# One GroupNorm evaluation per half-unit for both convolution stages of a ViT tokenizer on Trainium2

## The chip, the cores and the metric

The kernel runs on one core of one Trainium2 chip (trn2). The metric is the device time of one execution in microseconds (us); lower is better. The names of the engines in the rows are PE (TensorE matrix products), PEld (its weight loads), DVE (VectorE), ACT (ScalarE), POOL (GpSimd) and SP (the queue that issues DMAs).

## What is computed

A tokenizer over 784 patches (16 images, 7 x 7 patches of 3 x 16 x 16 pixels) feeds a small transformer. Only the tokenizer is touched here:

```python
x = _conv2d(x, conv1_w, conv1_b)              # 3 -> 64 channels, 3x3
residual = x
x = _group_norm(x, gn1_g, gn1_b)              # 32 groups of 2 channels, per patch
x = jax.nn.gelu(x, approximate=False)
x = _conv2d(x, rconv1_w, rconv1_b)            # 64 -> 64 channels, 3x3: the big one
x = _group_norm(x, gn2_g, gn2_b)
x = jax.nn.gelu(x, approximate=False)
x = _conv2d(x, rconv2_w, rconv2_b)
x = residual + x
x = _conv2d(x, proj_w, proj_b, stride=P, pad=0)   # 16x16 patch -> 192 numbers
```

The second residual convolution and the projection are folded into one weight (stage "fold"), so that what stands in the loop is: conv1, group norm 1, GELU 1, big convolution (`rconv1`), group norm 2, GELU 2, projection. The residual path is handled by another small product in the second half of the program.

## The kernel before, in words

**Tiling.** A unit is `U = 8` patches, a half is `Q = 4` patches; there are `UNITS = 98` units, so 196 halves, k = 2u + q with q = 0 or 1. Channels lie twice on the 128 partitions (odd and even rows of a patch), so a half of one stage is a PSUM bank of 128 x 512 numbers: `c1[q]` for conv1, `rc[p][q]` for the big convolution (p is the parity of the unit). Fourteen units make a group (`GU`), and there are seven groups. While group g runs through the convolutions, TensorE also projects group g-1: from the fifth half of a group on, every half carries 10 or 12 products of the projection (`project`), cut into 12 chunks of weights of which six units' worth are loaded again by DMA in every group. Group 0 has no projection beside it; the projection of group 6 stands alone after the loop. After it comes the second part of the program (`build_tail`), which the change leaves alone.

**What each engine does for a half k** (its emission or slot k); all five streams are written out by hand and only semaphores tie them together:

- TensorE, `emit`: 15 pairs of 64-column products of the big convolution of half k (lines 506 and 507; the two of a pair run side by side), with the projection's products (562, 566) strewn between them by `woven`. After pair 6 it waits for the copies of half k (`s_dup`), after pair 7 comes `means` of stage 1 for half k+3 (line 550, four small products that average the statistics of two channels), after pair 10 `conv1` of half k+4 into `c1[q]` (540, 541), which waits until GELU 1 of half k+2 has read that bank (`s_g1`), and after pair 13 of an even half `means` of stage 2 for the unit before. An emission starts only when `s_sp1` (split of half k done) and `s_g2` (GELU 2 of half k-4 done, the bank `rc` free) allow it.
- VectorE, `slot`: `channel_stats` of conv1 of half k+3 (four `bn_stats`, 777), `moments` of it (784 to 789), `channel_stats` of the big convolution of half k-1, `read_means` (793), `split1` of half k+2 (804 casts GELU 1 to the high 16 bits, 806 subtracts to get the low ones), in even halves `moments` of stage 2 over a whole unit, `split2` (813), in even halves `read_means` of stage 2.
- GpSimd, `norm(stage, ...)`: six or seven tiny operations in a chain (362, 363, 365, the power -0.5 in 367, 369, 371, 373) that turn averages into a scale `gsc` and a shift `gsh`. Per unit: stage 1 of four columns, stage 2 of eight columns, stage 1 of four columns.
- ScalarE: `gelu1` of half k+2 (420), then `gelu2_at` of half k-3 (429) and `hi2` (437, the high 16 bits of GELU 2).
- SP: per unit two loads of the im2col rows (254), per half four copies of `hst` into `acts` (274), and in groups 1 to 6 one chunk of the projection's weights (283).

All the statistics, averages, scales and shifts of stage 1 lie in buffers 0 and 1 (of four columns, in turn by half), those of stage 2 in buffers 2 and 3 (of eight columns, in turn by unit):

```python
N1, N2 = (0, 1), (2, 3)
wide = (Q, Q, U, U)
```

Of the kernel before, what the change touches and what calls it, by code (L numbers as in the profile page):

```python
# [28 lines left out]
HALF = 8 * P  # L29
# [22 lines left out]
MID = 48  # L52

# [15 lines left out]
def build_front(nc, a, emb, xs, ts, wrd):  # L69
# [9 lines left out]
    with ExitStack() as ctx:  # L79
# [25 lines left out]
        N1, N2 = (0, 1), (2, 3)  # L105
        wide = (Q, Q, U, U)
        bn6 = [sb(f"bn6_{s}", [128, w, 6]) for s, w in enumerate(wide)]
        ms = [sb(f"ms_{s}", [128, 2, w, 2]) for s, w in enumerate(wide)]
        msq = [sb(f"msq_{s}", [128, w, 2]) for s, w in enumerate(wide)]
        mst = [sb(f"mst_{s}", [128, 2, w]) for s, w in enumerate(wide)]  # L110
        tmp = [sb(f"tmp_{s}", [128, 5, w]) for s, w in enumerate(wide)]
        gsc = [sb(f"gsc_{s}", [128, w]) for s, w in enumerate(wide)]
        gsh = [sb(f"gsh_{s}", [128, w]) for s, w in enumerate(wide)]
        wid = sb("wid", [128, 2, 3, U])
# [57 lines left out]
        s_ms, s_st, s_rd = ([sem(f"{n}{s}") for s in (1, 2)] for n in ("moments", "group_means", "means_read"))  # L172
        s_dch, s_pch, s_sh = ([sem(f"{n}{s}") for s in (1, 2)] for n in ("dve_chain", "pool_chain", "affine"))
# [170 lines left out]
        def _(pool):  # L344
# [39 lines left out]
            norm(0, 0, 0)  # L384
            norm(0, 1, 1)
            norm(0, 0, 2)
            over_groups(pool, lambda g, b, first: over_units(pool, g, pair, first))
            norm(1, N2[1], UNITS - 1)

        @block.scalar  # L390
        def _(act):
# [48 lines left out]
            def group(g, b, first):  # L440
                def pair(u0, j, first, head):
                    for p in range(2):
                        u = u0 + p
                        for q in range(2):

                            gelu1(2 * u + 2 + q, q)
                            if first and 2 * p + q < 3:
                                continue
                            if head and 2 * p + q == 3:
                                act.wait_ge(s_pj, 1 if first else g)  # L450
                            uu, qq, pp = (u - 2, 1, p) if q == 0 else (u - 1, 0, 1 - p)
                            gelu2_at(uu, qq, pp)
                            old = head and 2 * p + q < 3
                            hi2(uu, qq, 1 - b if old else b, slot2(j, p, q, old))
# [1157 lines left out]
```

## Time and profile before

| | |
|---|---|
| median of three runs | 1846.43 us (1845.34 to 1847.88) |
| profiled execution, its own time | 1844.27 us |
| its span, first to last instruction | 1842.5 us |
| TensorE busy | 1513.2 us, 82% |
| VectorE busy | 1124.3 us, 61% |
| ScalarE busy | 850.0 us, 46% |
| GpSimd busy | 884.6 us, 48% |
| first conv1 of the loop to the last one (196 halves) | 269.4 to 1491.2 us |

The span is what the trace covers, the profiled execution's own time lies 1.8 us above it, and the median of the runs 2.2 us above that. Some 1222 us of it are the loop over the halves. An engine that is busy for 82% of the span is not thereby the bound: one has to see what the idle time of each engine in the loop waits for. Times of rows are in us from the start of the span, and one matrix product's own time (0.38 us) includes its way through the array, so the rate is read from start to start.

### The profile page before, as it was taken

What the parts mean: (1) busy time and instruction counts of PE and PEld (TensorE: products, weight loads), DVE (VectorE), ACT (ScalarE), POOL (GpSimd) and SP (SyncE); (2) the same over time, 40 slices, a digit from 0 to 9 for tenths busy, and PEclk for the clock granted to TensorE, in tenths of its full rate; (3) what the DMA queues carried; (4) which work ended last, traced back from release to release, by engine and by line L of the source; (5) the groups of instructions that cost most, each with busy time, mean ns of one, the idle gap of its engine ahead of it and who ended that gap; (6) DMA issues with size and microseconds to landing.
All of it is one profiled execution on the core that took longest, in us unless ns stands there. A gap on an engine that the chain in (4) does not pass through costs nothing. (4 is left out here: it accounts for less than half of the span.)

```text
span 1842.5 us, 45180 instructions
## 1 busy us (share of the span) xinstructions
PE 1513.2 (82%) x13782; PEld 1018.5 (55%) x13782; DVE 1124.3 (61%) x4307; ACT 850.0 (46%) x2118; POOL 884.6 (48%) x2190
## 2 busy tenths in 40 slices
PE   6879967666888788878888887888788857788999
PEld 3434423333666466646665665566566647656657
DVE  8533437767766766767767766667667653347330
ACT  1212225665555555555555555555555530243441
POOL 2000026666666666656666666666666640123410
PEclk9989979999999999989999999999999988786999
DMA  5643353323444344334434443444344465700000
GB/s 163 197 115 92 94 198 82 79 72 98 113 122 108 99 126 117 98 106 112 122 92 116 124 114 84 122 113 120 94 116 122 115 165 158 159 1 1 1 1 14
DMA packets 117232, 190.78 MB, mean 104 GB/s; under 512 B 18251, under 2 KB 86282, under 8 KB 116940
## 3 DMA queue, kind: packets, MB, share of 16 engines
q1 hardware_dynamic: 117068, 188.60, 37.5%
q8 instruction: 102, 1.67, 0.3%
q14 instruction: 62, 0.51, 0.1%
HBM read 103.34 MB, written 21.30 MB: 68 GB/s over the span
## 5 line engine op out<-in xcount | busy, mean ns | idle before, releaser
L506 PE MATMUL rc<-sb_acts,sb_rwd 128*64 128x512 f16 x1764 | 565.8, 393 | 4.7 <-DMA sb_acts<-sb_hst 4.7
L507 PE MATMUL rc<-sb_acts,sb_rwd 128*64 128x512 f16 x1764 | 566.9, 394 | 0.0
L506 PE MATMUL rc<-sb_acts,sb_rwl 128*64 128x512 f16 x1176 | 368.3, 395 | 111.9 <-ACT sb_g2f L429 78.8
L420 ACT ACTIVATE sb_f32q<-c,sb_gsh,sb_gsc 128x128 f32<-128x128 f32 x792 | 298.6, 458 | 308.8 <-POOL sb_gsh L373 308.8
L429 ACT ACTIVATE sb_g2f<-rc,sb_gsh,sb_gsc 128x128 f32<-128x128 f32 x784 | 296.5, 469 | 216.7 <-POOL sb_gsh L373 202.3
L367 POOL TENSOR_TENSOR sb_tmp<-sb_tmp,sb_half_neg 128x4 f32<-128x4 f32 (+1 forms) x297 | 371.0, 1249 | 23.5 <-POOL sb_tmp L365 0.5
L507 PE MATMUL rc<-sb_acts,sb_rwl 128*64 128x512 f16 x1176 | 369.7, 396 | 0.0
L813 DVE TENSOR_TENSOR sb_arena<-sb_g2f,sb_arena 128x512 f32 (+1 forms) x196 | 135.8, 693 | 326.6 <-ACT sb_arena L437 313.1
L362 POOL TENSOR_TENSOR sb_tmp<-sb_mst 128x4 f32<-128x4 f32 (+1 forms) x297 | 71.6, 241 | 545.3 <-DVE sb_mst L793 545.2
L562 PE MATMUL pj<-sb_wall,sb_arena 128*64 128x384 f16 x1792 | 306.0, 339 | 20.4 <-DMA sb_wall<-w_lo 11.3
L566 PEld LDWEIGHTS pj<-sb_wall,sb_arena 128*64 128x64 f16 x1792 | 213.3, 225 | 72.3 <-issue 2.4
L566 PE MATMUL pj<-sb_wall,sb_arena 128*64 128x192 f16 x1792 | 234.6, 248 | 0.0
L562 PEld LDWEIGHTS pj<-sb_wall,sb_arena 128*64 128x64 f16 x1792 | 210.1, 221 | 44.1 <-DMA sb_wall<-w_lo 12.8
L506 PEld LDWEIGHTS rc<-sb_acts,sb_rwl 128*64 128x64 f16 x1176 | 126.2, 110 | 177.5 <-issue 144.8
L481 PE MATMUL rc<-sb_acts,sb_arena 128*128 128x512 f16 x864 | 196.5, 385 | 29.3 <-DVE sb_acts L694 29.3
L506 PEld LDWEIGHTS rc<-sb_acts,sb_rwd 128*64 128x64 f16 x1764 | 170.8, 111 | 57.7 <-DMA sb_acts<-sb_hst 5.6
L550 PE MATMUL st<-sb_ms,sb_grp 128*64 128x16 f32 (+1 forms) x1188 | 86.0, 218 | 121.3 <-DVE sb_ms L789 120.4
L777 DVE BATCH_NORM_STATS2 sb_bn<-c 128x6 f32<-128x128 f32 x796 | 175.6, 283 | 7.2 <-issue 5.5
L550 PEld LDWEIGHTS st<-sb_ms,sb_grp 128*64 128x64 f32 x1188 | 66.0, 138 | 201.1 <-DVE sb_ms L789 125.0
L777 DVE BATCH_NORM_STATS2 sb_bn<-rc 128x6 f32<-128x128 f32 x784 | 173.8, 284 | 0.6 <-PE rc L507 0.6
L507 PEld LDWEIGHTS rc<-sb_acts,sb_rwd 128*64 128x64 f16 x1764 | 170.4, 111 | 0.5
L481 PEld LDWEIGHTS rc<-sb_acts,sb_arena 128*128 128x128 f16 x864 | 81.9, 97 | 135.5 <-issue 34.6
(161 smaller groups left out, 2310.2 us busy)
## 6 DMA issues: line engine op xcount, KB each, us to landing
sb_acts<-sb_hst SPq DMA_DIRECT2D x792, 78.8 KB, 2.1
sb_wall<-w_lo SPq DMA_DIRECT2D x56, 528.0 KB, 3.9
sb_im<-x_planes SPq DMA_DIRECT2D x202, 136.5 KB
sb_wall<-w_lo SPq DMA_DIRECT2D x28, 480.0 KB, 3.7
sb_f32q<-in_proj SPq DMA_DIRECT2D x12, 576.0 KB, 4.1
sb_arena<-in_proj SPq DMA_DIRECT2D x12, 576.0 KB, 4.4
w_lo<-sb_arena SPq DMA_DIRECT2D x1, 6144.0 KB, 17.3
scratch_fold<-sb_wall SPq DMA_DIRECT2D x48, 123.8 KB
```

The costliest lines, as they stand in the source:

```text
L362: ch.did(gp.tensor_tensor(t1, mean, mean, ALU.mult))
L367: ch.did(gp.tensor_tensor(t5, t3, half_neg[:, 0:w], ALU.pow))
L420: ins = nc.scalar.activation(g1f[:, q * Q + m, :], c1[q][:, m * HALF:(m + 1) * HALF], ACT.Gelu, bias=gsh[q][:, m:m + 1], scale=gsc[q][:, m ...
L429: ins = nc.scalar.activation(g2f[:, q * Q + m, :], rc[p][q][:, m * HALF:(m + 1) * HALF], ACT.Gelu, bias=gsh[s][:, q * Q + m:q * Q + m + 1] ...
L481: last = nc.tensor.matmul(out, w[:, wp, 3 * t + m, :], v[:, xp, t:t + 8, m * Q:(m + P) * Q], start=(n == 0), stop=(n == 17))
L506: nc.tensor.matmul(out[0:CH, :], w_odd, x_odd, start=(n == 0), stop=(n == 14))
L507: yield nc.tensor.matmul(out[CH:128, :], w_even, x_even, start=(n == 0), stop=(n == 14))
L550: last = nc.tensor.matmul(st[64 * h:64 * h + 64, 0:4 * wide[s]], grp[:, 64 * h:64 * h + 64], ms[s][:, :, :, :].rearrange("p a b k -> p (a ...
L562: last = nc.tensor.matmul(pj[at:at + 64, 0:2 * E], g2[:, b, 0, k:k + 64, n], both, start=(n == 0), stop=False)
L566: last = nc.tensor.matmul(pj[at:at + 64, 0:E], g2[:, b, 1, k:k + 64, n], whi[:, n, :], start=False, stop=(n == HALF - 1))
L777: v.bn_stats(bn6[s][:, at + m, :], src[:, m * HALF:(m + 1) * HALF]).then_inc(s_dch[stage_], 1)
L813: v.tensor_tensor(lo, src, hi, ALU.subtract).then_inc(s_sp2, 1)
```

## The change

One set of two buffers, each eight columns wide, takes the place of the four. Buffer s holds in columns 0 to 3 the statistics of conv1 of half n = k+3 and in columns 4 to 7 those of the big convolution of half n-4 = k-1. `moments`, `means`, `read_means` and `norm` run once a half over the eight columns; `wid` and `wid2` hold the parameters of stage 1 in the first four columns and of stage 2 in the last four.

- VectorE's slot becomes: statistics of the big convolution of half k-1, statistics of conv1 of half k+3, `moments`, `split2` of half k-3, `read_means`, `split1` of half k+2.
- TensorE's emission has one `means`, after pair 10 (`MEANS_AT`), and `conv1` after pair 13 (`CONV1_AT`).
- GpSimd has one eight-wide `norm` a half, with two more waits ahead of the write to `gsc` (until the GELUs that read that buffer's old values are done).
- ScalarE does `gelu2_at` and `hi2` of half k-3 ahead of `gelu1` of half k+2; GELU 2 of a half reads columns 4 to 7 of buffer q and waits for norm 2u+q+5.
- At the start the parameters are spread with a few more small VectorE operations, and the first three norms are eight wide.

```diff
+MEANS_AT, CONV1_AT = 10, 13
...
-            def norm(stage_, s, n):
+            def norm(n, s, guard=True):
...
-                pool.wait_ge(s_rd[stage_], n + 2)
+                pool.wait_ge(s_rd, n + 2)
...
+                if guard:
+                    pool.wait_ge(s_g1, n - 1)
+                    pool.wait_ge(s_g2, n - 1)
                 ch.did(gp.tensor_tensor(gsc[s][:, :], t5, gam, ALU.mult))
...
-                    norm(0, 1, 2 * u + 3)
-                    if not (first and p == 0):
-                        norm(1, N2[1 - p], u - 1)
-                    norm(0, 0, 2 * u + 4)
+                    for q in range(2):
+                        norm(2 * (u0 + p) + q + 3, 1 - q)
...
             def gelu2_at(u, q, p):
-                s = N2[p]
-                act.wait_ge(s_sh[1], u + 1)
+                act.wait_ge(s_sh, 2 * u + q + 5)
...
+                                gelu2_at(uu, qq, pp)
+                                old = head and 2 * p + q < 3
+                                hi2(uu, qq, 1 - b if old else b, slot2(j, p, q, old))
                             gelu1(2 * u + 2 + q, q)
...
-            def means(stage_, s, n, other):
-
-                pe.wait_ge(s_ms[stage_], n + 1)
-                pe.wait_ge(s_rd[stage_], n + 1)
-                pe.wait_ge(s_rd[1 - stage_], other + 1)
+            def means(n, s):
+
+                pe.wait_ge(s_ms, n + 1)
+                pe.wait_ge(s_rd, n + 1)
...
                 pe.wait_ge(s_dup[p][q], 64 * (pairs_done + 1))
-                woven(1)
-                means(0, N1[1 - q], 2 * u + q + 3, u - (q == 0) if k2 else 0)
-                woven(3)
+                woven(MEANS_AT - 6)
+                means(2 * u + q + 3, 1 - q)
+                woven(CONV1_AT - MEANS_AT)
                 if q == 0:
                     pe.wait_ge(s_im[p], 32 * (pairs_done + 2))
                 pe.wait_ge(s_g1, 2 * u + q + 3)
                 conv1(q, p)
-                woven(3)
-                if q == 0 and k2:
-                    means(1, N2[1 - p], u - 1, 2 * u + q + 4)
-                woven(2).then_inc(s_rc, 1)
+                woven(15 - CONV1_AT).then_inc(s_rc, 1)
...
+                    if seen:
+                        dve.wait_ge(s_rc, k)
+                        channel_stats(1 - q, rc[p][0] if q == 1 else rc[1 - p][1], Q)
                     dve.wait_ge(s_c1, k + 5)
-                    channel_stats(0, N1[1 - q], c1[1 - q], 0)
-                    moments(0, N1[1 - q], 7 * (k + 3) + 4)
...
-                    read_means(0, N1[1 - q], k + 3)
-                    split1(k + 2, q, 1 - p, pair_at + 1)
-                    if q == 0 and n2:
-                        moments(1, N2[1 - p], 11 * (u - 1) + 8)
-
+                    channel_stats(1 - q, c1[1 - q], 0)
+                    moments(k + 3, 1 - q, 11 * k + 25 if seen else 25)
                     if not (first and p == 0) and not (first and p == 1 and q == 0):
                         old = head and 2 * p + q < 3
                         split2(k - 3, 1 - q, 1 - b if old else b, slot2(j, p, q, old))
-                    if q == 0 and n2:
-                        read_means(1, N2[1 - p], u - 1)
+                    read_means(k + 3, 1 - q)
+                    split1(k + 2, q, 1 - p, pair_at + 1)
```

How the rows stand on the engines that the prediction speaks of. First VectorE, in the last loop over units, an even half before (777 is `bn_stats`, 784 to 789 `moments`, 793 `read_means`, 804 and 806 `split1`, 813 `split2`):

```order
L777 BN_STATS sb_bn_1<-c_1 128x6 x4
...
L784 TENSOR_SCALAR sb_ms<-sb_bn_1,sb_par 128x8
...
L777 BN_STATS sb_bn_2<-rc 128x6 x4
...
L793 TENSOR_REDUCE sb_mst<-st 128x8
L804 CAST sb_hst<-sb_f32q 128x4x8x16
L806 TENSOR_TENSOR sb_acts<-sb_f32q,sb_hst 128x4x8x16
...
L784 TENSOR_SCALAR sb_ms<-sb_bn_2,sb_par 128x16
...
L813 TENSOR_TENSOR sb_arena<-sb_g2f,sb_arena 128x512
L793 TENSOR_REDUCE sb_mst<-st 128x16
```

And the same place now (770 is `bn_stats`, 777 to 782 `moments`, 786 `read_means`, 797 and 799 `split1`, 806 `split2`):

```order
L770 BN_STATS sb_bn_1<-rc 128x6 x4
...
L770 BN_STATS sb_bn_1<-c_1 128x6 x4
...
L777 TENSOR_TENSOR sb_ms<-sb_bn_1,sb_wid 128x16
...
L806 TENSOR_TENSOR sb_arena<-sb_g2f,sb_arena 128x512
...
L786 TENSOR_REDUCE sb_mst<-st 128x16
...
L797 CAST sb_hst<-sb_f32q 128x4x8x16
L799 TENSOR_TENSOR sb_acts<-sb_f32q,sb_hst 128x4x8x16
```

The second `moments` and the second `read_means` are gone, the statistics of the big convolution stand first, and `split2` moved ahead of `read_means`, `split1` to the end.

TensorE in an even half with projection, before, around the two products of `means` and `conv1` (550 is `means`, 540 `conv1`, 506 and 507 a pair, 562 and 566 the projection):

```order
L550 MATMUL st<-sb_ms,sb_grp 64x16 x2
L506 MATMUL rc<-sb_acts,sb_rwd 64x512
L507 MATMUL rc<-sb_acts,sb_rwd 64x512
...
L540 MATMUL c_0<-sb_im,sb_w1s 64x512
L541 MATMUL c_0<-sb_im,sb_w1s 64x512
...
L550 MATMUL st<-sb_ms,sb_grp 64x32 x2
```

And now (546 is `means`, 537 `conv1`, 503 and 504 a pair, 558 and 562 the projection):

```order
L546 MATMUL st<-sb_ms,sb_grp 64x32 x2
L503 MATMUL rc<-sb_acts,sb_rwd 64x512
L504 MATMUL rc<-sb_acts,sb_rwd 64x512
...
L558 MATMUL pj<-sb_wall,sb_arena 64x384 x2
...
L537 MATMUL c_0<-sb_im,sb_w1s 64x512
L538 MATMUL c_0<-sb_im,sb_w1s 64x512
```

One `means` stands where two stood, three pairs later than the first of them, and `conv1` three pairs later too.

## Rows read from the trace of the kernel before

**Rows 1.** TensorE's line 541 by window: busy us (x halves), granted clock, DMA:
```profile
269.30:438.00 168.70, 10.97 (x28) 3.15 (x29) 0.99 0.30 78
269.30:1491.30 1222.00, 75.12 (x196) 21.23 (x196) 0.99 0.40 107
```
**Rows 2.** Waits of TensorE in the loop: total us, times, longest:
```profile
PE st L550 <- DVE sb_ms L789: 111.2, 181, 4.1
PE rc L506 <- ACT sb_g2f L429: 78.8, 59, 2.2
```
**Rows 3.** Timeline, TensorE, one unit: start, length, instruction [idle before <-releaser]:
```profile
1001.56 0.38 PE L506 MATMUL rc<-sb_acts,sb_rwl 128*64 128x512 f16 x1 [0.55 <-issue]
...
1008.00 0.38 PE L506 MATMUL rc<-sb_acts,sb_rwl 128*64 128x512 f16 x1
...
1010.31 0.25 PE L550 MATMUL st<-sb_ms,sb_grp 128*64 128x16 f32 x4
...
1011.32 0.38 PE L540 MATMUL c<-sb_im,sb_w1s 108*64 108x512 f16 x1
...
1012.47 0.41 PE L506 MATMUL rc<-sb_acts,sb_rwd 128*64 128x512 f16 x1
...
1013.10 0.26 PE L566 MATMUL pj<-sb_wall,sb_arena 128*64 128x192 f16 x2
1014.24 0.40 PE L506 MATMUL rc<-sb_acts,sb_rwl 128*64 128x512 f16 x1 [0.88 <-ACT sb_g2f L429]
```
**Rows 4.** The same unit on VectorE:
```profile
1002.49 0.70 DVE L813 TENSOR_TENSOR sb_arena<-sb_g2f,sb_arena 128x512 f32 x1 [3.00 <-ACT sb_arena L437]
...
1004.02 0.23 DVE L784 TENSOR_SCALAR sb_ms<-sb_bn,sb_par 128x8 f32<-128x8 f32 x1
...
1004.58 0.88 DVE L777 BATCH_NORM_STATS2 sb_bn<-rc 128x6 f32<-128x128 f32 x4
...
1005.45 0.42 DVE L804 CAST sb_hst<-sb_f32q 128x512 f16<-128x512 f32 x1
1005.91 0.71 DVE L806 TENSOR_TENSOR sb_acts<-sb_f32q,sb_hst 128x512 f16<-128x512 f32 x1
...
1007.95 0.18 DVE L793 TENSOR_REDUCE sb_mst<-st 128x16 f32<-128x32 f32 x1
```
**Rows 5.** The same unit on ScalarE:
```profile
1001.60 0.63 ACT L437 ACTIVATE sb_arena<-sb_g2f 128x512 f32 x1
...
1012.50 1.51 ACT L429 ACTIVATE sb_g2f<-rc,sb_gsh,sb_gsc 128x128 f32<-128x128 f32 x4 [2.23 <-POOL sb_gsh L373]
```
**Rows 6.** The same unit on GpSimd:
```profile
1006.16 0.52 POOL L365 TENSOR_TENSOR sb_tmp<-sb_mst,sb_tmp 128x4 f32<-128x4 f32 x1
...
1008.60 0.20 POOL L362 TENSOR_TENSOR sb_tmp<-sb_mst 128x8 f32<-128x8 f32 x1
1008.76 0.20 POOL L363 TENSOR_TENSOR sb_tmp<-sb_mst,sb_wid 128x8 f32<-128x8 f32 x1
...
1012.26 0.20 POOL L373 TENSOR_TENSOR sb_gsh<-sb_wid,sb_tmp 128x8 f32<-128x8 f32 x1
```
**Rows 7.** GpSimd, the last norm of the loop, VectorE idle beside it:
```profile
1499.00 0.20 POOL L363 TENSOR_TENSOR sb_tmp<-sb_mst,sb_wid 128x8 f32<-128x8 f32 x1
...
1501.84 0.20 POOL L373 TENSOR_TENSOR sb_gsh<-sb_wid,sb_tmp 128x8 f32<-128x8 f32 x1
```
**Rows 8.** Timeline, SP's queue, four copies of one half and the copy kind's landing:
```profile
1023.61 2.38 SPq L274 DMA_DIRECT2D sb_acts<-sb_hst  x4
```
**Rows 9.** The page, DMA issues: count, KB each, median us from issue to landing:
```profile
sb_acts<-sb_hst SPq DMA_DIRECT2D x792, 78.8 KB, 2.1
```
**Rows 10.** Timeline, VectorE: first operation of group 5, behind its loop's branch:
```profile
1144.15 0.89 DVE L777 BATCH_NORM_STATS2 sb_bn<-c 128x6 f32<-128x128 f32 x4 [2.70 <-issue]
```
**Rows 11.** Timeline, TensorE, from the loop's last emission to the last projection:
```profile
1497.72 0.43 PE L550 MATMUL st<-sb_ms,sb_grp 128*64 128x32 f32 x4 [4.66 <-DVE sb_ms L789]
1507.08 0.62 PE L562 MATMUL pj<-sb_wall,sb_arena 128*64 128x384 f16 x2 [8.94 <-DVE sb_arena L813]
```

More of the change, by code:

```diff
@@ L103, in build_front @@
         par = sb("par", [128, 7])
[L105 to L114, printed above, removed]
+        bn6 = [sb(f"bn6_{s}", [128, U, 6]) for s in range(2)]
+        ms = [sb(f"ms_{s}", [128, 2, U, 2]) for s in range(2)]
+        msq = [sb(f"msq_{s}", [128, U, 2]) for s in range(2)]
+        mst = [sb(f"mst_{s}", [128, 2, U]) for s in range(2)]
+        tmp = [sb(f"tmp_{s}", [128, 5, U]) for s in range(2)]
+        gsc = [sb(f"gsc_{s}", [128, U]) for s in range(2)]
+        gsh = [sb(f"gsh_{s}", [128, U]) for s in range(2)]
+        wid = sb("wid", [128, 3, U])
+        wid2 = sb("wid2", [128, U, 2])
         zeros = sb("zeros", [128, U])
@@ L444, in pair @@
                         for q in range(2):
-                            gelu1(2 * u + 2 + q, q)
[L447 to L454, printed above, removed]
+                            if not (first and 2 * p + q < 3):
+                                if head and 2 * p + q == 3:
+                                    act.wait_ge(s_pj, 1 if first else g)
+                                uu, qq, pp = (u - 2, 1, p) if q == 0 else (u - 1, 0, 1 - p)
+                                gelu2_at(uu, qq, pp)
+                                old = head and 2 * p + q < 3
+                                hi2(uu, qq, 1 - b if old else b, slot2(j, p, q, old))
+                            gelu1(2 * u + 2 + q, q)
                 pair(g * GU, 0, first, True)
@@ L576, in emit @@
             def emit(u, q, p, g, b, first, pairs_done, s_idx=None):
-                k2 = not (first and p == 0)
                 pe.wait_ge(s_sp1, 2 * u + q + 1)
@@ L645, in _ @@
             conv1(1, 0)
-            means(0, 0, 0, 0)
-            means(0, 1, 1, 0)
+            means(0, 0)
+            means(1, 1)
             pe.wait_ge(s_im[1], 32)
@@ L650, in _ @@
             conv1(0, 1)
-            means(0, 0, 2, 0)
+            means(2, 0)
             pe.wait_ge(s_g1, 2)
@@ L654, in _ @@
             over_groups(pe, group)
-            means(1, N2[1], UNITS - 1, 2 * UNITS + 3)
+            means(2 * UNITS + 3, 1)
             for c in range(NCH):
@@ L862, in _ @@
             dve.wait_ge(s_c1, 2)
[L863 removed]
+            channel_stats(0, c1[0], 0)
             moments(0, 0, 4)
             dve.wait_ge(s_c1, 3)
[L866 to L869 removed]
+            channel_stats(1, c1[1], 0)
+            moments(1, 1, 11)
+            read_means(0, 0)
+            read_means(1, 1)
             split1(0, 0, 0, None)
             dve.wait_ge(s_c1, 4)
[L872 to L874 removed]
+            channel_stats(0, c1[0], 0)
+            moments(2, 0, 18)
+            read_means(2, 0)
             split1(1, 1, 0, None)
@@ L885, in _ @@
             dve.wait_ge(s_rc, K)
-            channel_stats(1, N2[1], rc[1][1], Q)
-            moments(1, N2[1], 11 * (UNITS - 1) + 8)
-            read_means(1, N2[1], UNITS - 1)
+            channel_stats(1, rc[1][1], Q)
+            dve.wait_ge(s_c1, K + 5)
+            channel_stats(1, c1[1], 0)
+            moments(K + 3, 1, 11 * K + 25)
+            read_means(K + 3, 1)
             for k in (K - 3, K - 2, K - 1):
```

85 lines of the change are left out of this document (35 added, 50 removed).

## The prediction

> **What bounds the kernel now.** I read the windows by line first: 28 conv1 of group 0 lie 168.7 us apart in all, 196 of the whole loop 1222 us [rows 1], so a half costs 6.0 us without a projection beside it and 6.2 over all. Adding the projection's products costs almost nothing, so TensorE's work is not the bound. The list of waits says who is: 111 us for the moments of VectorE and 79 us for GELU 2, in the loop alone [rows 2]. The timeline of one unit gives TensorE's own pace. An odd half runs without a wait from 1008.00 to the last product at 1013.10 and 0.09 beyond, 5.19 us, and the whole unit takes 1001.56 to 1014.24 = 12.68 [rows 3]. The even half has two projection products less (384 and 192 columns, 0.16 and 0.08 us at the granted 2.4 GHz, share 0.99 [rows 1]), hence 4.95. The four chunks of ten in twelve take another 0.24 a unit off: on average 10.06 a unit, **5.03 a half**, against some 6.3 spent.
>
> What closes the loop is one ring a unit, and it is seen by following who ends each wait: `hi2` at 1001.60 [rows 5]; `split2` at 1002.49, which VectorE stood 3.00 us for; statistics, moments, split and at last the stage 2 `read_means` at 1007.95 [rows 4]; the eight-wide norm 1008.60 to 1012.46 [rows 6]; GELU 2 at 1012.50 to 1014.01 [rows 5]; TensorE's next even half at 1014.24, 0.88 idle for just that [rows 3]. From 1001.60 to the next `hi2`, 0.12 behind 1014.01, is 12.5 us: the period. It passes VectorE, GpSimd and ScalarE one after the other, so each is idle half the time and yet together they set the pace.
>
> **What is removed and added.** Per unit one `moments`, one `means` and one `read_means` of three go, and two norms of four columns and one of eight become two of eight. What counts is not their busy time but where the ring now closes. I set out one half, t = 0 at the start of emission k, P the period.
>
> 1. The big convolution of half k-1 is done near t = 0.1. Statistics of it and of conv1, 0.88 each, with hand-overs 1.8; moments 0.56 (1004.02 to 1004.58) [rows 4]. The averages can start at 2.5. TensorE gets there after ten pairs: `conv1` stood behind ten pairs at 1011.32, 3.32 from 1008.00, and 0.08 of that is the old `means` (1010.31, four products, next start 0.08 on) [rows 3]: 3.24. The wait for moments goes, with 0.7 to spare.
> 2. `means` 0.25 and 0.04, `read_means` 0.18 [rows 3, 4]: read at 3.71. `split2` (0.70) lies ahead of it, from 2.4 to 3.1, free: its input was ready long before, see 4.
> 3. The norm, N. Bare it takes 1499.00 to 1502.04 and 0.16 for its first step, **3.20** [rows 6, 7]. In the ring it took 1008.60 to 1012.46, **3.86** [rows 6], because VectorE's `split1` ran into it: line 365 takes 0.52 instead of 0.20 when it meets line 806 (1005.91 to 1006.62) and ends 0.06 behind it [rows 4, 6]. Now `split1` starts together with the norm or up to 0.4 us behind, so something of this stays; the power, which is more than half of N, outlasts it. I take N = 3.4, ends 3.2 and 3.9.
> 4. GELU 1 starts 0.04 behind the norm and takes 1.51, GELU 2 of half k-4 another 1.5, `hi2` 0.63 [rows 5]. ScalarE has 3.9 us of work a half, below P. GELU 1 of half k+2 is done at 3.76 + N + 1.55 - P = 8.7 - P, so at 3.6 for P = 5.07. GELU 2 is done 1.5 later, in emission k, and TensorE wants it at emission k+2: the 79 us go.
> 5. `conv1` comes behind pair 13: the row at 1012.47, less the old `conv1` (0.23), 4.24 [rows 3]. Needed: GELU 1 by then. From `means` to the next half's `conv1` there are P + 1.00; the chain takes 0.29 + 0.18 + 0.05 + N + 0.04 + 1.51 + 0.05 = N + 2.12. So **P >= N + 1.12**: 4.52 at N = 3.4, 4.98 at 3.86. Below 5.03, but closely.
> 6. VectorE's own ring: `read_means` of half n, norm, GELU 1, `split1` (1.17 with its cast at 1005.45 to 1006.62), then statistics 1.8, moments 0.56, `split2` 0.61, the next but one `read_means`: 0.18 + 0.05 + N + 0.04 + 1.51 + 0.05 + 1.17 + 1.8 + 0.56 + 0.61, that is 5.97 + N for two halves [rows 4 to 7]. **P >= 4.7** at N = 3.4; 4.6 to 4.9 for its ends.
> 7. The copies of a half: the cast ends near 4.6 in slot k-2, four issues take 2.38, the last lands 2.1 after its issue [rows 8, 9], so at 9.1; emission k wants them behind pair 6, near 2P + 1.9 = 12. 2.9 us to spare. The im2col loads and chunks share the queue, and a unit still has 10 us.
>
> So with the projection beside it a half becomes TensorE's: 5.03, and I take **5.07** since single halves may meet point 5. Without it (28 halves of group 0, four at the head of each later group, 52 in all) TensorE would need less than 4 us, and point 6 gives **4.7**.
>
> **The sum.** 143 x 5.07 = 725; 52 x 4.7 = 244; two passes over the outer loop's branch, where VectorE stood 2.70 us [rows 10] and nothing covers it: 5.4; for the token outputs at six group ends and some microseconds at 1.2 GHz behind them I allow 9. In all 984, against 1222 [rows 1]: 238 less. Outside the loop: from the end of the last emission (1497.72 - 4.66 = 1493.06) to the first product of the last projection (1507.08) are 14.0 us [rows 11]; the new order has one GELU 2 left there instead of two: 1.8 + 0.56 + 0.5 + N (bare) 3.2 + 1.51 + 0.8 + 0.8 = 9.2, 4.8 less. At the start three norms grow from four columns to eight; the two that stand in line cost some 2 us. 1844.3 - 238 - 4.8 + 2 = 1603.5, and the median of the runs lay 2.2 above the profiled execution: **1606**. With N = 3.2 and 5.03 a half it is 1595; with N = 3.9 (4.94 and 5.1) it is 1623.
>
> **A row that speaks against it.** Point 3 rests on one reading: a GpSimd operation that meets line 806 only ends late, it does not lose the whole overlap. No row shows the power beginning under `split1`. Were it held for the full cast and subtraction, 0.42 + 0.71 [rows 4], then N = 4.33. The Trainium skill, GPSIMD Engine Reference, section "Key points", says that GpSimd shares its SBUF interfaces with VectorE and contends with instructions of a 2-port mode or with two SBUF inputs, which both parts of `split1` may be. The 0.52 agrees that there is contention; how much of a long operation it costs no row here shows. By the page, with the whole overlap lost, the sum would be that of the first rival below.
>
> **The rivals.**
> - *The norm is held for all of `split1`.* N = 4.33, so P = 5.45 with the projection and (5.97 + 4.33) / 2 = 5.15 without: 779 + 268 + 14 = 1061, 161 less. **1683.** For it: the collision is now in every half. Against it: a held operation ends 0.06 behind VectorE's, so its reading and its work were done under the hold.
> - *Another wait takes the place.* The queue of SP is the candidate: a copy has 2.9 us to spare, and all 16 DMA engines will be busier (0.40 of the span now [rows 1]) in less time. If the copies came late by so much that P stayed at 5.75, the loop would give back 0.68 x 143 = 97 us; at 6.2, and 5.2 without the projection, 162 + 26 = 188: **1703 to 1794**. Against it: the margin of point 7.
> - *Slower: the merged norm stands on the path of both stages.* GELU 1 now waits for statistics of the big convolution that it never needed. If not only `split1` but all of VectorE's work held GpSimd (0.42 + 0.71 + 0.70 + 1.76 + 0.56 = 4.15), N would be 7.35, P = 8.5 and 6.7: 1215 + 348 + 14, **about 2195**. It is slower than before from N = 5.3 on. Against it: line 362 took 0.20 at 1008.60 [rows 6], where VectorE, done with `read_means` at 1008.13 [rows 4], was at the next half's `bn_stats`, so these don't hold it.
> - *No change.* A ring that I don't see closes at 6.2. The order of rows shows that the old one is cut, so this is a residue.
>
> **How the numbers follow.** The forecast (1583 to 1630) 0.67; norm held (1630 to 1695) 0.16; another wait (1695 to 1840) 0.09; no change 0.02; slower 0.06. The likeliest is 1606. The range takes the first two cases, 1583 to 1695. Faster by over 0.2% (about what a measurement of this kernel can tell from none): 0.92; within it 0.02; slower 0.06.
>
> **What the changed kernel's profile would show.** Conv1 to conv1 5.0 to 5.2 us with the projection, even and odd halves nearly alike, and 4.6 to 4.9 in group 0; TensorE waits for neither moments nor GELU 2; GpSimd starts its norm each half near 3.8 us behind TensorE's start and takes 3.2 to 3.9; ScalarE has about 1.2 us idle a half. I am wrong at point 3 if the power row takes over 1.9 us; at point 5 if line 537 waits for GELU 1; at point 7 if the first pair behind pair 6 waits for a DMA; at point 1 if `means` still waits for moments.

## The result and the profile after

| | before | changed |
|---|---|---|
| median of four runs | 1847.16 us (1845.34 to 1849.16) | **1636.3 us** (1624.12 to 1637.54) |
| profiled execution, its own time / span | 1844.27 / 1842.5 us | 1635.12 / 1633.3 us |
| ratio to before, 95% interval | | 0.8843 (0.88 to 0.8887) |
| first conv1 of the loop to the last | 1222 us | 1012 us (271.5 to 1283.5) |

In a later session the same kernel took 1628.62 us, ratio 0.8853 (0.8824 to 0.8882). The time is inside the range, 30 us above the forecast of 1606. It lies in the band (1630 to 1695) that the prediction had set apart for its first rival with a chance of 0.16, 6 us above the forecast's own band, and not because that rival's mechanism came true; the later session's 1628.62 lies in the forecast's band.

The page of the changed kernel, busy time by engine and the landing of the copies (median in the last column, against 2.1 in [rows 9]):

```profile
PE 1467.2 (90%) x13394; PEld 1002.0 (61%) x13394; DVE 1086.1 (66%) x3830; ACT 837.3 (51%) x2118; POOL 713.5 (44%) x1511
...
sb_acts<-sb_hst SPq DMA_DIRECT2D x792, 78.8 KB, 2.6
```

Line 538 (conv1's second product) by window, the answer to [rows 1]: group 0, the whole loop, and a stretch with the projection. 28 halves now lie 141.7 us apart in all instead of 168.7, all 196 take 1012 instead of 1222:

```profile
271.40:413.10 141.70, 11.25 (x29) 3.03 (x29) 1.00 0.36 92
271.40:1283.40 1012.00, 76.96 (x195) 20.93 (x195) 0.99 0.48 129
900.00:990.00 90.00, 6.68 (x17) 1.82 (x17) 1.00 0.52 139
```

Waits of TensorE in the loop, the answer to [rows 2] (total us, times, longest). The 111 us for moments are 12.3, the 79 us for GELU 2 are gone; what is left is 37.7 us for GELU 1 at conv1, in 26 places, nearly all in group 0 and the group heads (the first four halves of a group, which have no projection yet). The list has only waits in which TensorE stood idle:

```profile
PE c L537 <- ACT sb_f32q L419: 37.7, 26, 1.6
PE st L546 <- DVE sb_ms L782: 12.3, 33, 1.3
PE rc L503 <- issue: 6.9, 2, 3.7
PE rc L503 <- DMA sb_acts<-sb_hst: 4.3, 12, 0.8
```

**With the projection** a half is nearly TensorE's own. From 900 to 960 us it was busy all of the 60.00 us at a granted clock of 1.00, and conv1 follows conv1 by 5.09 and 5.13 in turn. Even so, every second conv1 there was released by GELU 1:

```profile
908.73 0.41 PE L537 MATMUL c<-sb_im,sb_w1s 108*64 108x512 f16 x1
```
```profile
907.18 1.50 ACT L419 ACTIVATE sb_f32q<-c,sb_gsh,sb_gsc 128x128 f32<-128x128 f32 x4 [2.14 <-POOL sb_gsh L375]
```

GELU 1 ended at 908.68 and conv1 began 0.05 behind it, 1.08 behind `means` (907.65). All 66 such halves that I counted have this 0.05, and conv1 comes 1.11 behind `means` in them (median), 1.02 in the others, where GELU 1 ends 0.77 before it. The product ahead was still running, so this wait of 0.1 is in no list of idle time. GpSimd and VectorE there; start, length, instruction. The power (line 366) begins under the cast of `split1`, runs on under its subtraction and takes 1.70, against 1.64 where no 128x512 instruction of VectorE overlaps it:

```profile
908.94 1.70 POOL L366 TENSOR_TENSOR sb_tmp<-sb_tmp,sb_half_neg 128x8 f32<-128x8 f32 x1
...
908.71 0.43 DVE L797 CAST sb_hst<-sb_f32q 128x512 f16<-128x512 f32 x1 [0.57 <-ACT sb_f32q L419]
909.18 0.70 DVE L799 TENSOR_TENSOR sb_acts<-sb_f32q,sb_hst 128x512 f16<-128x512 f32 x1
```

The norm took 3.24 there (908.23 to 911.47) and 3.92 in the next half (913.42 to 917.34).

**In group 0** the steady halves take 4.2 or 4.3 and 5.9 us in turn, because only every second norm stands in the ring. GpSimd's norm of one half, and the next one's first step:

```profile
366.39 0.31 POOL L361 TENSOR_TENSOR sb_tmp<-sb_mst 128x8 f32<-128x8 f32 x1 [2.51 <-DVE sb_mst L786]
366.67 0.19 POOL L362 TENSOR_TENSOR sb_tmp<-sb_mst,sb_wid 128x8 f32<-128x8 f32 x1
366.94 0.53 POOL L364 TENSOR_TENSOR sb_tmp<-sb_mst,sb_tmp 128x8 f32<-128x8 f32 x1
367.55 1.64 POOL L366 TENSOR_TENSOR sb_tmp<-sb_tmp,sb_half_neg 128x8 f32<-128x8 f32 x1
...
369.84 0.71 POOL L375 TENSOR_TENSOR sb_gsh<-sb_wid,sb_tmp 128x8 f32<-128x8 f32 x1
370.67 0.20 POOL L361 TENSOR_TENSOR sb_tmp<-sb_mst 128x8 f32<-128x8 f32 x1
```

And VectorE over the same two halves, `read_means` to the next but one `read_means` (line 786):

```profile
366.13 0.18 DVE L786 TENSOR_REDUCE sb_mst<-st 128x16 f32<-128x32 f32 x1
366.23 0.42 DVE L797 CAST sb_hst<-sb_f32q 128x512 f16<-128x512 f32 x1
366.68 0.73 DVE L799 TENSOR_TENSOR sb_acts<-sb_f32q,sb_hst 128x512 f16<-128x512 f32 x1
...
369.80 0.69 DVE L806 TENSOR_TENSOR sb_arena<-sb_g2f,sb_arena 128x512 f32 x1 [0.17 <-issue]
...
372.30 0.43 DVE L797 CAST sb_hst<-sb_f32q 128x512 f16<-128x512 f32 x1 [1.71 <-ACT sb_f32q L419]
...
373.38 0.88 DVE L770 BATCH_NORM_STATS2 sb_bn<-rc 128x6 f32<-128x128 f32 x4
...
375.83 0.69 DVE L806 TENSOR_TENSOR sb_arena<-sb_g2f,sb_arena 128x512 f32 x1 [0.15 <-issue]
376.44 0.18 DVE L786 TENSOR_REDUCE sb_mst<-st 128x16 f32<-128x32 f32 x1
```

The ring of point 6 is there: 366.13 to 376.44 = 10.31 for two halves. Its parts are 0.26 to the norm, 4.16 norm, 1.75 to `split1`, 1.08, statistics 1.70, moments with the gap behind them 0.75, `split2` 0.61. Forecast were 0.23, 3.4, 1.60, 1.17, 1.80, 0.56, 0.61 = 9.37. The norm alone is 0.76 over, and its rows say why: three of its small steps, 0.20 each by themselves, took 0.31, 0.53 and 0.71, and each ends 0.05 or 0.06 behind a VectorE instruction of 128x512: the cast, the subtraction of `split1`, and `split2`. So `split1` took 0.44 from this norm, where 0.2 was forecast, and `split2` 0.51, where nothing was. The next norm (370.67 to 374.08) took 3.41, and TensorE did not wait for it.

**The end of the loop**, the answer to [rows 11]:

```profile
1287.64 0.31 PE L546 MATMUL st<-sb_ms,sb_grp 128*64 128x32 f32 x4 [3.16 <-DVE sb_ms L782]
1295.26 0.62 PE L558 MATMUL pj<-sb_wall,sb_arena 128*64 128x384 f16 x2 [7.32 <-DVE sb_arena L806]
```

From the last emission's end (1287.64 - 3.16) to the first product are 10.8 us instead of 14.0.

### The profile page after: what moved, and what is told of

It reads as the page before. It is cut to its first block and busy times, and to the rows that moved or that the text cites. A ratio compares the mean times of both kernels' runs of the same rounds, so it can differ in the third digit from the quotient of the medians.

```text
span 1633.3 us, 42631 instructions
## 1 busy us (share of the span) xinstructions
PE 1467.2 (90%) x13394; PEld 1002.0 (61%) x13394; DVE 1086.1 (66%) x3830; ACT 837.3 (51%) x2118; POOL 713.5 (44%) x1511
## 5 line engine op out<-in xcount | busy, mean ns | idle before, releaser
L366 POOL TENSOR_TENSOR sb_tmp<-sb_tmp,sb_half_neg 128x8 f32<-128x8 f32 x200 | 335.3, 1677 | 15.7
L558 PE MATMUL pj<-sb_wall,sb_arena 128*64 128x384 f16 x1792 | 300.8, 339 | 20.7 <-DMA sb_wall<-w_lo 13.4
L361 POOL TENSOR_TENSOR sb_tmp<-sb_mst 128x8 f32<-128x8 f32 x200 | 58.4, 292 | 530.5 <-DVE sb_mst L786 528.8
L562 PEld LDWEIGHTS pj<-sb_wall,sb_arena 128*64 128x64 f16 x1792 | 210.8, 226 | 75.6 <-issue 0.5
L558 PEld LDWEIGHTS pj<-sb_wall,sb_arena 128*64 128x64 f16 x1792 | 208.1, 223 | 41.2 <-DMA sb_wall<-w_lo 14.6
L562 PE MATMUL pj<-sb_wall,sb_arena 128*64 128x192 f16 x1792 | 230.9, 248 | 0.0
L503 PEld LDWEIGHTS rc<-sb_acts,sb_rwd 128*64 128x64 f16 x1764 | 180.4, 110 | 69.1 <-DMA sb_acts<-sb_hst 13.0
L504 PEld LDWEIGHTS rc<-sb_acts,sb_rwd 128*64 128x64 f16 x1764 | 180.3, 110 | 4.0
L806 DVE TENSOR_TENSOR sb_arena<-sb_g2f,sb_arena 128x512 f32 (+1 forms) x196 | 135.8, 693 | 28.8 <-issue 12.8
L797 DVE CAST sb_hst<-sb_f32q 128x512 f16<-128x512 f32 x198 | 85.3, 431 | 93.2 <-ACT sb_f32q L419 92.2
L799 DVE TENSOR_TENSOR sb_acts<-sb_f32q,sb_hst 128x512 f16<-128x512 f32 x198 | 141.1, 713 | 6.8
## 6 DMA issues: line engine op xcount, KB each, us to landing
w_lo<-sb_arena SPq DMA_DIRECT2D x1, 6144.0 KB, 17.3
```

What stands on the lines that cost most here:

```text
L366: ch.did(gp.tensor_tensor(t5, t3, half_neg[:, :], ALU.pow))
L503: nc.tensor.matmul(out[0:CH, :], w_odd, x_odd, start=(n == 0), stop=(n == 14))
L504: yield nc.tensor.matmul(out[CH:128, :], w_even, x_even, start=(n == 0), stop=(n == 14))
L558: last = nc.tensor.matmul(pj[at:at + 64, 0:2 * E], g2[:, b, 0, k:k + 64, n], both, start=(n == 0), stop=False)
L562: last = nc.tensor.matmul(pj[at:at + 64, 0:E], g2[:, b, 1, k:k + 64, n], whi[:, n, :], start=False, stop=(n == HALF - 1))
L797: v.tensor_copy(hi, src).then_inc(s_sp1h, 1)
```

## The experiments

Two theories came out of this. *Bounds*: with the projection a half takes the larger of TensorE's pace and N + 1.12 (point 5); without it, half of 5.97 + N (point 6). *Hold*: N is 3.2 plus what VectorE's 128x512 instructions take from it, and `split2` in its new place is one of them. The rivals were that something else (the copies, the clock, the places of `means` and `conv1`) sets those halves. The table has, worked out from the starts of conv1, the steady time of **two** halves in group 0 and with the projection. Each ratio is to the kernel before, timed again in the same session.

| kernel | group 0 | with projection | median us | ratio to before (95%) |
|---|---|---|---|---|
| before | 12.3 | 12.6 | 1847 | 1 |
| changed | 4.2 + 5.9 | 5.09 + 5.13 | 1636.3 | 0.8843 (0.88 to 0.8887) |
| e1, `split2` behind `read_means` | 10.05 | 5.13 + 5.58 | 1667.0 | 0.9044 (0.9003 to 0.9085) |
| e2, norm longer | 11.2 | 5.05 + 6.3 | 1735.8 | 0.9426 (0.9379 to 0.9473) |
| e3, before, stage 2 norm longer | 12.8 | 12.85 | 1880.86 | 1.0212 (1.0151 to 1.0273) |
| e4, earlier places | 10.4 | 5.44 + 5.44 | 1675.02 | 0.9103 (0.9058 to 0.9149) |
| e5, GELU 1 first | 17.3 | 8.6 + 8.7 | 2291.96 | 1.2437 (1.2372 to 1.2501) |
| e6, stage 1's columns first | 9.4 | 5.02 + 5.11 | **1602.33** | 0.871 (0.8675 to 0.8744) |
| e7, `split2` between statistics | 10.75 | 5.1 + 5.7 | 1675.43 | 0.9091 (0.9058 to 0.9123) |
| e8, e6 and e7 together | 10.25 | 5.0 + 5.25 | 1632.59 | 0.8852 (0.8818 to 0.8887) |
| e9, as e6, all on GpSimd | 9.85 | 5.0 + 5.1 | 1611.8 | 0.875 (0.8715 to 0.8786) |
| e10, e1 with conv1 at 14 | 10.0 | 5.0 + 5.3 | 1643.14 | 0.8902 (0.8863 to 0.8941) |

The changed kernel itself took 1636.3 us in one session and 1628.62 in another at nearly the same ratio (0.8843 and 0.8853), so a difference between medians of two sessions can be off by some 8 us.

### e1: split2 behind read_means

```diff
                     moments(k + 3, 1 - q, 11 * k + 25 if seen else 25)
+                    read_means(k + 3, 1 - q)
                     if not (first and p == 0) and not (first and p == 1 and q == 0):
                         old = head and 2 * p + q < 3
                         split2(k - 3, 1 - q, 1 - b if old else b, slot2(j, p, q, old))
-                    read_means(k + 3, 1 - q)
                     split1(k + 2, q, 1 - p, pair_at + 1)
```

> The changed kernel with one edit: VectorE's split2 stands behind read_means and ahead of split1, instead of ahead of read_means. Theory (split2 holds the norm of the half before and lies on VectorE's ring in the 52 halves without a full projection beside them): a half without projection falls from 5.06 to about 4.5 to 4.7 us, the norm there from 4.16 to about 3.7, halves with the projection stay at 5.1 since TensorE is their bound; in all about 20 us less than the changed kernel, 1610 to 1620. Rival (these halves are held by something else, the clock or the copies): no change, 1630 to 1640. Second rival (split2 now meets the start of every norm and only moves the hold, while split1 waits 0.6 longer): slower, 1640 to 1660.

Measured: 1667.0. The direction is that of the second rival, the size is past it. Group 0 gained some 0.15 in two halves; every second half with the projection went from 5.1 to 5.58, which the first theory had left out. GpSimd and VectorE there:

```profile
926.21 0.20 POOL L361 TENSOR_TENSOR sb_tmp<-sb_mst 128x8 f32<-128x8 f32 x1 [1.90 <-DVE sb_mst L786]
926.37 0.68 POOL L362 TENSOR_TENSOR sb_tmp<-sb_mst,sb_wid 128x8 f32<-128x8 f32 x1
...
927.46 2.10 POOL L366 TENSOR_TENSOR sb_tmp<-sb_tmp,sb_half_neg 128x8 f32<-128x8 f32 x1
...
926.29 0.69 DVE L806 TENSOR_TENSOR sb_arena<-sb_g2f,sb_arena 128x512 f32 x1 [0.16 <-issue]
...
927.37 0.70 DVE L799 TENSOR_TENSOR sb_acts<-sb_f32q,sb_hst 128x512 f16<-128x512 f32 x1
```

`split2` now meets the norm's start instead of its end (0.68 instead of 0.20), and `split1`, pushed back by it, meets the start of the power: 2.10 instead of 1.64. The norm took 926.21 to 930.59 = 4.38, and N + 1.12 = 5.50 against 5.58 measured. The hold was moved, not removed. TensorE waited for GELU 1 in 101 places instead of 26. So point 5's bound is real, and the changed kernel stood on it in every second half with the projection: 3.92 + 1.12 = 5.04 against 5.11.

### e2 and e3: a longer norm

e2 does one small step of the norm four times instead of once, 0.84 us more with the same result; e3 does so in the kernel before, in the stage 2 norm alone.

```diff
-                ch.did(gp.tensor_tensor(t3, sq, t1, ALU.subtract))
-                ch.wait()
+                for _ in range(4):
+                    ch.did(gp.tensor_tensor(t3, sq, t1, ALU.subtract))
+                    ch.wait()
```

> The changed kernel with the third step of GpSimd's norm (t3 = sq - t1, 8 columns, same result) done four times instead of once: each norm longer by three such steps, about 0.84 us from the distance of two steps in the trace (0.28). Theory (a half with the projection needs P = N + 1.12, a half without (5.97 + N) / 2 plus the hold): with N about 4.1 to 4.7, halves with projection go from 5.12 to 5.4 to 5.6, those without by 0.42, so 143 x 0.4 + 52 x 0.42, some 60 to 80 us more: 1695 to 1715. Rival (TensorE alone bounds the halves with projection and there is 0.8 to spare): only the 52 halves pay, 22 us: about 1658.

Measured: 1735.8, 99 us more, where the theory had 60 to 80. GpSimd's norm in one of the longer halves, and TensorE's wait behind it:

```profile
950.55 0.44 POOL L361 TENSOR_TENSOR sb_tmp<-sb_mst 128x8 f32<-128x8 f32 x1 [2.33 <-DVE sb_mst L787]
...
954.52 0.58 POOL L372 TENSOR_TENSOR sb_gsc<-sb_tmp,sb_wid 128x8 f32<-128x8 f32 x1 [0.22 <-POOL sb_tmp L367]
...
957.34 0.41 PE L538 MATMUL c<-sb_im,sb_w1s 108*64 108x512 f16 x1 [1.16 <-ACT sb_f32q L420]
```

This norm took 5.12 (to 955.67), since its later steps now meet `split2` (0.58): 5.12 + 1.12 = 6.24, measured 6.3. The next, 955.63 to 959.66, took 4.03, which asks for 5.15, and TensorE's own 5.05 to 5.1 was kept. Group 0 grew by 13.4 us over 28 halves, 0.48 each, where point 6 asks for half of 0.84, 0.42. The rival, slack of over 0.84 with the projection, is out.

> The kernel before with the same three extra steps (0.84 us) in the stage 2 norm alone, the eight-wide one of each unit; the result is the same. Theory (one ring a unit passes through that norm once and sets 12.5 us a unit): 98 units x 0.84 = 82 us more, about 1929. Rival (the ring is not what bounds the unit, the norm has slack): under 20 us more, 1847 to 1867.

Measured: 1880.86, 40 us more, between both; from two runs, 1.5% to 2.7% slower. The loop (1232 to 1261 us, from one conv1 ahead) took 29 of the 39 us between the two traces, 0.25 to 0.5 a unit. Some 2 lie before it, and most of the rest lies near the end, in `build_tail`, which this edit leaves alone: the granted clock was 0.82 and 0.84 in two stretches there (1759 to 1796 and 1796 to 1829 us), where the kernel before had 1.00 and 0.89 (1728 to 1758 and 1758 to 1790). So that part is no price of the norm. The ring of [rows 3 to 6] does pass through this norm, but the added 0.84 came through as 0.28 in it, because the power and the step behind it no longer meet `split1`, and the unit grew by about as much. Before (first row) one took 0.67, with the longer norm (second) 0.20:

```profile
936.04 0.67 POOL L369 TENSOR_TENSOR sb_gsc<-sb_tmp,sb_wid 128x8 f32<-128x8 f32 x1
```
```profile
968.65 0.20 POOL L370 TENSOR_TENSOR sb_gsc<-sb_tmp,sb_wid 128x8 f32<-128x8 f32 x1
```

The norm took 3.78 before (933.49 to 937.27) and 4.06 here (965.35 to 969.41), the unit 12.6 and 12.85.

### e4: earlier places

```diff
-MEANS_AT, CONV1_AT = 10, 13
+MEANS_AT, CONV1_AT = 7, 10
```

> The changed kernel with means behind pair 7 instead of 10 and conv1 behind pair 10 instead of 13 (MEANS_AT, CONV1_AT = 7, 10); the distance between them is the same. Theory (only the wait for moments, ready some 2.5 us into a half, is late against the earlier place at 2.3, and the chain from means to conv1 one half on is as long as before): 0 to 15 us more, 1636 to 1651. Rival (the places are essential: moments are later than 2.5, and each half then waits for them in the open): over 30 us more, above 1666.

Measured: 1675.02, 39 us more, the rival. A half with the projection takes some 5.4; the waits for moments in the loop rose from 12.3 to 45.9 us:

```profile
PE st L546 <- DVE sb_ms L782: 45.9, 57, 2.0
```

The expectation contradicted the prediction's own number. Point 1 gave moments 0.7 us to spare, and the changed kernel's trace has that (moments done at 912.13, `means` at 912.84: 0.71). Three pairs with their products are 0.96, so each half had to pay some 0.3, and it did.

### e5: ScalarE's old order

```diff
+                            gelu1(2 * u + 2 + q, q)
                             if not (first and 2 * p + q < 3):
...
                                 hi2(uu, qq, 1 - b if old else b, slot2(j, p, q, old))
-                            gelu1(2 * u + 2 + q, q)
```

> The changed kernel with ScalarE's old order in a half: GELU 1 first, then GELU 2 of half k-3 and its rounded copy (hi2). Theory (split2 stands ahead of read_means, so GELU 2 behind GELU 1 closes a ring of one half: read_means 0.2, norm 3.3, GELU 1 1.5, GELU 2 1.4, hi2 0.8, split2 0.6 and hand-overs): a half takes 7.9 us, the kernel 2100 to 2200, slower than before. Rival (point 4 of the prediction: GELU 2 has emissions to spare, so its place on ScalarE does not matter): within 0.5% of the changed kernel, 1628 to 1645.

Measured: 2291.96, the theory, past its 2100 to 2200: a half takes 8.6 instead of 7.9. The order of the two GELUs is worth some 655 us. VectorE, then ScalarE:

```profile
906.00 0.69 DVE L806 TENSOR_TENSOR sb_arena<-sb_g2f,sb_arena 128x512 f32 x1 [4.49 <-ACT sb_arena L435]
906.61 0.18 DVE L786 TENSOR_REDUCE sb_mst<-st 128x16 f32<-128x32 f32 x1
```
```profile
902.15 1.51 ACT L419 ACTIVATE sb_f32q<-c,sb_gsh,sb_gsc 128x128 f32<-128x128 f32 x4 [5.03 <-POOL sb_gsh L375]
903.54 1.52 ACT L427 ACTIVATE sb_g2f<-rc,sb_gsh,sb_gsc 128x128 f32<-128x128 f32 x4
905.18 0.64 ACT L435 ACTIVATE sb_arena<-sb_g2f 128x512 f32 x1
```

GELU 1 to `split2` are 3.85, `split2` over `read_means` and the norm to the next GELU 1 (910.64) 4.64: 8.49, a ring of one half. So "GELU 2 has emissions to spare" holds only because it runs ahead of GELU 1; `split2` stands before `read_means` on VectorE, and that chains stage 2's copy to stage 1's norm.

### e7: split2 between the two statistics

```diff
                         channel_stats(1 - q, rc[p][0] if q == 1 else rc[1 - p][1], Q)
                     dve.wait_ge(s_c1, k + 5)
-                    channel_stats(1 - q, c1[1 - q], 0)
-                    moments(k + 3, 1 - q, 11 * k + 25 if seen else 25)
                     if not (first and p == 0) and not (first and p == 1 and q == 0):
                         old = head and 2 * p + q < 3
                         split2(k - 3, 1 - q, 1 - b if old else b, slot2(j, p, q, old))
+                    channel_stats(1 - q, c1[1 - q], 0)
+                    moments(k + 3, 1 - q, 11 * k + 25 if seen else 25)
```

> The changed kernel with split2 moved between the statistics of the big convolution and those of conv1, where GpSimd's power is under way. Theory (an operation that begins under VectorE's two-input subtraction is held to its end, one already under way is not): the 0.5 us hold at the end of every second norm of group 0 (L375, 0.71 instead of 0.20) goes, the two halves fall from 10.15 to some 9.65, heads by as much, projection halves stay at 5.12 or the odd ones gain a hold and reach 5.2: 1622 to 1632. Rival (the moments are now too late for means, as with the earlier places): 5.3 a half, above 1650.

Measured: 1675.43, the rival. The last step of the norm is bare now (line 375, 0.20; line 371 still meets `split2` in every second norm of group 0, 0.40 to 0.43), but in group 0 `split2` begins after an idle time of 0.3 to 0.5 and stands ahead of the moments, and `split1` meets the power's start in every steady half there. The second row is TensorE's waits for moments in the loop, 81.5 us instead of 12.3:

```profile
368.87 2.09 POOL L366 TENSOR_TENSOR sb_tmp<-sb_tmp,sb_half_neg 128x8 f32<-128x8 f32 x1
```
```profile
PE st L546 <- DVE sb_ms L782: 81.5, 117, 1.6
```

e1 and e7 together say that the changed kernel's place for `split2` is the best of the three: the last thing before the chain needs VectorE again.

### e10: the bound of point 5 and conv1's place

e1 with `MEANS_AT, CONV1_AT = 10, 14`.

> The kernel with split2 behind read_means (1667 us; its odd projection halves took 5.58 us, held by GELU 1 at conv1, its even ones 5.12), with conv1 behind pair 14 instead of 13. Theory (a half needs the norm's length plus 1.12 us less whatever conv1 moves back): the odd halves gain one pair with its products, 0.33 us, and take 5.25, the even ones stay: 72 x 0.33 = 23 us less, some 1643. Rival (the odd halves are held by something else, or conv1's statistics now come too late for means): 1660 or more.

Measured: 1643.14, the theory; the long halves 5.3, waits for GELU 1 in the loop 24 us in 47 places instead of 56 in 101. The bound of point 5 moves with conv1 as worked out.

### e6, e8, e9: GELU 1's columns first

If the 52 halves are set by the chain through GpSimd, it should pay to keep the shared statistics and means but to release GELU 1 before stage 2's columns are done. e6 cuts the norm in two that way and moves two of its steps (mean squared and variance) to VectorE; e9 cuts it in the same way and leaves these two steps on GpSimd; e8 is e6 with `split2` placed as in e7. The edit of e6:

```diff
-                ch.did(gp.tensor_tensor(t1, mean, mean, ALU.mult))
                 ch.did(gp.tensor_tensor(t2, mean, bias, ALU.subtract))
...
+                pool.wait_ge(s_vr, 2 * n + 2)
+                for half, done in ((slice(0, Q), s_sh), (slice(Q, U), s_sh2)):
+                    ch.did(gp.tensor_tensor(t5[:, half], t3[:, half], half_neg[:, half], ALU.pow))
+                    ch.wait()
...
+                    gp.tensor_tensor(gsh[s][:, half], bet[:, half], t4[:, half], ALU.subtract).then_inc(done, 1)
...
             def gelu2_at(u, q, p):
-                act.wait_ge(s_sh, 2 * u + q + 5)
+                act.wait_ge(s_sh2, 2 * u + q + 5)
...
             def read_means(n, s):
...
+                ch.did(v.tensor_tensor(t1, mean, mean, ALU.mult))
+                ch.wait()
+                ch.did(v.tensor_tensor(t3, sq, t1, ALU.subtract))
```

> The changed kernel with statistics and means still shared, but the norm cut in two on GpSimd: power, scale and shift of stage 1's four columns first, which release GELU 1, then stage 2's four with a semaphore of their own for GELU 2; mean squared and variance move to VectorE behind read_means (2 operations, some 0.4 us). From the rows GELU 1 is released some 2.6 us behind the start of read_means instead of 3.5 to 4.4. Theory (the halves without a full projection are set by the chain through GpSimd, those with it by TensorE): 5.07 falls to 4.6 to 4.7 in group 0 and 5.3 to about 4.9 in the group heads, others stay at 5.12: 1610 to 1620. Rival (GpSimd, now busy 4.1 us a half and held at times, or VectorE with 0.4 more becomes the bound): 1635 to 1670.

Measured: **1602.33**, ratio 0.871 (0.8675 to 0.8744) against 0.8843 (0.88 to 0.8887) of the changed kernel: 1.5% faster than it, and under the expected 1610 to 1620. Group 0 has 4.7 a half as expected, the projection halves 5.02 and 5.11, and the wait for GELU 1 is gone from the loop. What bounds group 0 now is read from one window of it (PE, PEld, DVE, ACT, POOL busy us of 80, then clock and DMA), first the changed kernel, then e6, then e9:

```profile
320.00:400.00 80.00, 63.32 (x566) 28.47 (x566) 63.44 (x253) 55.28 (x144) 51.40 (x109) 1.00 0.35 91
```
```profile
320.00:400.00 80.00, 67.65 (x616) 31.54 (x612) 74.21 (x309) 61.65 (x154) 66.60 (x155) 1.00 0.39 99
```
```profile
320.00:400.00 80.00, 66.99 (x590) 28.34 (x586) 66.67 (x263) 59.27 (x147) 68.21 (x178) 1.00 0.37 94
```

VectorE is at 74 of 80 in e6, with nothing but short hand-overs left.

> The changed kernel with the norm cut in two on GpSimd (power, scale and shift of stage 1's four columns first, then stage 2's), but mean squared and variance stay on GpSimd, so VectorE gets no work more. With the earlier variant VectorE was busy without a pause in group 0, 4.7 us a half. Theory (VectorE's own work set those 4.7): 0.4 less on VectorE against 0.5 more on GpSimd, 4.5 to 4.7 in group 0 and projection halves as there, 1595 to 1610. Rival (GpSimd, now some 4.4 us of work a half plus a hold of 0.5, is the bound): 4.9 to 5.0 in group 0 and 5.1 to 5.2 with the projection, 1615 to 1640.

Measured: 1611.8, between the two. Without VectorE's two extra steps group 0 is slower, 4.9 to 4.95 a half, as the rival says, while the projection halves are as in e6. The same window shows GpSimd the busiest engine (68.21), and its trace has one norm following the other without a pause: here GpSimd is the bound of group 0. So the two steps on VectorE keep GpSimd from being that bound in e6; whether VectorE alone sets e6's 4.7 is not shown.

> The last two edits together: stage 1's columns first on GpSimd, and split2 between the statistics. Theory: as the first of them, with less hold at the norm's end: 1605 to 1618. Rival (VectorE's extra 0.4 and split2 ahead of the moments make means late, or GpSimd is the bound): 1640 to 1680.

Measured: 1632.59, between the theory and the rival: e7's place for `split2` costs 30 us here as it cost 39 there.

> The changed kernel itself, beside the others on the same chip: 1636 us (1630 to 1640) if the time repeats.

Measured: 1628.62 (1624.74 to 1639.04), ratio 0.8853: the time repeats within 0.5%, its ratio within 0.1 points, and e6 and e9 are faster than it by more than the intervals.

## Why the prediction was right, and what was off

- **The bound before** was read rightly: with the ring cut, 210 us of the loop went, and the waits for moments and GELU 2 with it. e3 shows that the ring passes through the stage 2 norm: that norm grew by 0.28 net and the unit by 0.25. The edit merges the norms, closes stage 2 once a half and moves `means`, `conv1` and the splits, all at once; the places were varied one by one, the merging was never taken out alone, so its own share is not known.
- **Point 1** (moments 0.7 to spare): 0.71 in the trace, and e4 pays when three pairs are taken away.
- **Point 3** (N = 3.4, ends 3.2 and 3.9): 3.24 and 3.92 in turn with the projection; in group 0 3.4, and 4.16 for the norms in the ring, past the upper end. The first rival, a power held for all of `split1`, did not happen: 1.70, not 2.8.
- **Point 2** is the step that failed: "`split2` (0.70) lies ahead of it, from 2.4 to 3.1, free". Its input is ready, and for TensorE it is free. But it falls on the last steps of the norm of the half before (0.71 instead of 0.20), and I had counted only `split1` as a holder. With the holds by `split1`, 0.24 more than forecast, this makes the norm of the ring 0.76 longer than 3.4 in group 0; in the group heads such norms take 3.9 to 4.5. That it was `split2` is read from rows: e1 and e7 moved it, but other holds took its place, so no run has the changed kernel without this hold alone.
- **The term 52 x 4.7** is therefore the one that was mis-sized: 244 forecast, 268.9 measured (141.6 in group 0, 127.3 in the heads of groups 1 to 6), some 25 of the 28 us that the loop is over. In group 0 the longer norm accounts for it: 0.38 a half over 28 halves is 10.6 us, and 10 were measured above 28 x 4.7.
- **The term 143 x 5.07** was nearly right: 743.1 with the branches, against 739 with all allowances. The pace is 5.11; 0.1 of two halves is the wait for GELU 1, for e6, where GELU 1 ends over 1 us before conv1, has 5.02 and 5.10. The two passes over the outer branch cost 3.9 each instead of 2.7 (intervals of 9.3 and 8.8).
- **Points 4 to 7**: by its own sign (line 537 waits for GELU 1) point 5 is not quite met: GELU 1 is late in group 0 and, by 0.1, in every second half with the projection. e1, e2 and e10 put the bound at N + 1.12 within 0.1, all of them on its upper side. The copies were late in 12 places for 4.3 us in all, although their landing went from 2.1 to 2.6 us.
- **Outside the loop**: 3.2 us less to the last projection instead of 4.8, and in all only 1.5 from the last conv1 to the span's end; the start cost 2.1 as said.
- **The number** is better than its parts: the range held since it also took in the first rival, whose mechanism did not happen.

## What to carry to other kernels

When two small chains are merged into one wide step, ask which consumer can least afford the wider step and release it first: e6 keeps all the merging and gives GELU 1 its four columns early. Count the engines that share a resource with the chain in every place where they now run side by side; moving such an instruction moves its toll and seldom removes it. And an order that looks like a detail (GELU 2 ahead of GELU 1) can be what keeps two rings apart.

## What the runs showed of the hardware

**VectorE first.** A GpSimd operation that began while VectorE ran a 128x512 cast or subtraction ended late, whatever its own length. The changed kernel's loop has some 240 small steps (0.20 alone) that began at least 0.15 ahead of such an instruction's end: they took 0.27 to 0.74 and all ended 0.04 to 0.07 behind it. The power of eight columns (1.64 alone) ended 1.49 behind it: 1.70 to 1.92 long in 71 cases of the changed kernel that began under the cast, 2.07 to 2.11 in some 80 of e1 that began under the subtraction. The power of four columns (1.01 alone) ended 0.86 behind it in e6. In all three the operation ends its own length less 0.15 behind VectorE's instruction. Steps that met only statistics or moments took 0.20 to 0.26.

**GpSimd first.** A power that had begun before a subtraction was not held by it: 1.64 in 26 cases. It did not hold VectorE either: 74 subtractions of the changed kernel ran wholly under a power (71 of these powers had been held by the cast just before) and took 0.696, the 98 `split2` with no GpSimd beside them 0.692. Only a subtraction that began within 0.025 of a small step's start was slower, 0.73 in 97 cases; those that began 0.05 or more behind it took 0.69.

The Trainium skill, SBUF — State Buffer, section "SBUF: two separate sides", says of VectorE instructions in a 2-port mode or with two SBUF inputs that whichever of the two engines starts first has the shared port pair for its whole instruction and that the other blocks fully. The runs agree for VectorE first, and the measurement decides against it for GpSimd's power first, which did not block VectorE for its whole length.

The power of eight columns took 1.64, of four 1.01, so cutting it in two costs 0.38.
